# Latent attention on one core: each unit's value matmuls as a run of their own, ten runs a pair of heads in place of five

## What is computed

```python
def _L1_attn_ref(x, latent_w, latent_b, Wd_w, Wd_b, out_w, out_b):
    Wdkv = x @ latent_w + latent_b                                    # 36 latents per token: keys and values
    q = jnp.einsum('btc,hcl->bhtl', x, Wd_w) + Wd_b[None, :, None, :] # 16 heads
    scores = jnp.einsum('bhtl,bsl->bhts', q, Wdkv) / jnp.asarray(np.sqrt(d_head), dtype=x.dtype)
    scores = jnp.where(causal[None, None, :, :], scores, -jnp.inf)
    attn = jax.nn.softmax(scores, axis=-1)
    y = jnp.einsum('bhts,bsl->bhtl', attn, Wdkv)
    z = jnp.transpose(y, (0, 2, 1, 3)).reshape(b, t, h * Wdkv.shape[-1])
    return z @ out_w + out_b
...
x = x + _L1_attn_ref(_layernorm(x, axis=-1), L1_attn_latent_w, ...)
```

## Time and profile before

| | us |
|---|---|
| median of 3 runs | 3037.49 (3032.99 to 3039.72) |
| the profiled execution, its own time | 3026.82 |
| span of that execution in the trace | 3025.1 |
| latent attention's pairs and outputs in it | about 2061 to 2911 |
| granted clock of PE, mean, as a share of 2.4 GHz | 0.941 |

### The profile page before, as it was taken

The page is one execution under the profiler, slowest core; times in us unless marked ns, Lnnn a source line. Parts: engine busy times, 40 slices in busy tenths (PEclk is TensorE's granted clock), DMA queues, the critical chain, the costliest instruction groups (busy, mean ns, idle before and its releaser), DMA issues. The chain is left out here.

```text
span 3025.1 us, 53686 instructions
## 1 busy us (share of the span) xinstructions
PE 2700.4 (89%) x15208; PEld 1865.9 (62%) x15208; DVE 2011.5 (66%) x5083; ACT 1140.5 (38%) x2101; POOL 887.8 (29%) x1203
## 2 busy tenths in 40 slices
PE   7999999967887888779999999778998988999989
PEld 5888888844554555458888888534455455455454
DVE  6777777747778687667777777545655555556542
ACT  3111111116666666621111111234544544544544
POOL 3223223315655555532223233001111111111200
PEclk9999999968989889879999999888999999999999
DMA  3000000000000000020000000001110110111100
GB/s 137 0 0 0 0 0 0 0 1 2 3 3 3 3 3 2 2 101 1 0 0 0 0 0 1 1 4 45 37 37 26 37 37 26 37 37 28 46 2 28
DMA packets 31976, 52.01 MB, mean 17 GB/s; under 512 B 8178, under 2 KB 14066, under 8 KB 31732
## 3 DMA queue, kind: packets, MB, share of 16 engines
q1 hardware_dynamic: 27124, 41.88, 4.5%
q0 software_dynamic: 4608, 7.09, 0.9%
HBM read 17.93 MB, written 2.10 MB: 7 GB/s over the span
## 5 line engine op out<-in xcount | busy, mean ns | idle before, releaser
L616 DVE SCALAR_TENSOR_TENSOR moe_acc<-moe_ps,moe_comb,moe_acc 128x512 f32<-128x512 f32 x896 | 660.9, 744 | 155.1 <-PE moe_ps L322 152.1
L2221 DVE CUSTOM_DVE_ANT_0 attn_masked<-attn_psm,attn_causal 128x1024 f32<-128x1024 f32 (+1 forms) x504 | 363.1, 757 | 259.0 <-PE attn_psm L1903 258.4
L2118 ACT ACTIVATE attn_probs<-attn_pse 128x512 f32<-128x512 f32 (+1 forms) x640 | 314.1, 557 | 341.7 <-PE attn_pse L1918 339.3
L322 PE MATMUL moe_ps<-moe_Wg,moe_xh 128*128 128x512 f32 x1024 | 328.9, 403 | 19.0 <-DVE moe_Wg L539 19.0
L353 PE MATMUL moe_ps<-moe_Wd,moe_ih 128*128 128x512 f32 x1024 | 341.6, 415 | 3.4 <-DVE moe_Wd L539 3.4
L322 PE MATMUL moe_ps<-moe_Wu,moe_xh 128*128 128x512 f32 x1024 | 332.8, 406 | 3.1 <-POOL moe_Wu L477 3.1
L1830 POOL TENSOR_SCALAR_AFFINE_SELECT attn_probs<-attn_probs 128x256 f32<-128x256 f32 (+1 forms) x192 | 95.0, 495 | 709.1 <-ACT attn_probs L2118 709.0
L1934 PE MATMUL attn_psy<-attn_probs,attn_V 128*64 128x512 f32 (+3 forms) x1536 | 290.6, 508 | 0.0
L487 POOL TENSOR_SCALAR moe_part<-consts,moe_pick,moe_prob 128x8 f32<-128x8 f32 x256 | 97.4, 394 | 625.5 <-ACT moe_prob L410 625.5
L1115 POOL TENSOR_TENSOR attn_R<-attn_R 128x1024 f32<-128x1024 f32 (+1 forms) x128 | 213.6, 1680 | 188.4 <-DVE attn_R L1463 188.4
L1903 PE MATMUL attn_psm<-attn_kS,attn_qS 108*128 108x512 f32 (+3 forms) x672 | 197.9, 395 | 48.5 <-DVE attn_mx L2221 42.5
(11 more groups left out here) (228 smaller groups left out, 4755.7 us busy)
## 6 DMA issues: line engine op xcount, KB each, us to landing
attn_qS<-attn_qH SPq DMA_DIRECT2D x192, 72.0 KB
attn_qS<-attn_qL SPq DMA_DIRECT2D x96, 72.0 KB
attn_qS<-attn_qH POOLq DMA_DIRECT2D x64, 72.0 KB, 2.1
moe_stageg<-in_w_gate SPq DMA_DIRECT2D x8, 512.0 KB, 7.3
moe_stageu<-in_w_up SPq DMA_DIRECT2D x8, 512.0 KB, 7.2
moe_stageg<-in_w_down SPq DMA_DIRECT2D x8, 512.0 KB, 3.6
attn_qS<-attn_qL POOLq DMA_DIRECT2D x32, 72.0 KB, 2.5
out<-X SPq DMA_DIRECT2D x8, 256.0 KB, 2.4
```

The source lines that it names most:

```text
L322: last = pe.matmul(expert_bank[j % 4][:, :], a[q][:, :], w[b][:, cols], start=k == 0, stop=k == 2)
L616: dve.scalar_tensor_tensor(acc[:, q, r, :], expert_bank[j % 4][:, :], comb[:, q, r, e:e + 1], acc[:, q, r, :], ALU.mult, ALU.add).then_inc ...
L2118: act.activation(probs[:, ring(q, u), c, HALF - n:HALF], e_part(k, HALF - n, HALF), ACT.Exp, scale=SCORE_SCALE).then_inc(p_ready, 1)
L2221: dve.tensor_tensor_reduce(masked[:, 0 if j >= 4 else 1, 0:n], max_part(k, 0, n, spare), causal[:, SEQ - n:SEQ], 1.0, NEG, ALU.add, ALU.ma ...
```

## The change

A step's run of two units is parted. The unit of even number is put behind the step's first two scores, ahead of the third; the unit of odd number stays at the step's end. This holds for `d == 0` too, whose two units are those of the pair before (no such units where `i == 0`). In the last step that puts unit 6 ahead of the transpose and the projection, and leaves unit 7 behind them. Nothing is added or left out: the same matmuls on the same tiles with the same waits. The last pair of an element keeps units 8 and 9 behind unit 7.

```diff
-                        for u, c in ((2 * d, 0), (2 * d, 1), (2 * d + 1, 0)):
-                            scores(m, q, u, c)
+                        for c in range(2):
+                            scores(m, q, 2 * d, c)
+                        if d >= 1:
+                            values(m, q, 2 * d - 2)
+                        elif i > 0:
+                            values(m - 1, 1 - q, NU - 2)
+                        scores(m, q, 2 * d + 1, 0)
...
                         if d == 0:
                             if i > 0:
-                                for u in (NU - 2, NU - 1):
-                                    values(m - 1, 1 - q, u)
+                                values(m - 1, 1 - q, NU - 1)
...
                         else:
-                            for u in (2 * d - 2, 2 * d - 1):
-                                values(m, q, u)
+                            values(m, q, 2 * d - 1)
```

## The result

The changed kernel takes **3102.03 us** (median of 4 runs, 3096.98 to 3107.18) where the kernel before takes 3035.24 beside it: +66.8 us, a ratio of 1.0221 with a 95% interval of [1.0204, 1.0237]. Slower was forecast, by 56 us, at 3093 in a range of 3064 to 3120. The profiled execution took 3096.98, its span is 3095.2.

A forecast was written before the change was run, and what follows sets the result against it. PE's fixed order was taken to set the pace, with a DMA floor behind the transpose. Inner pairs gave 21 x 2.1 = 44 us, other pairs 4 + 4 + 4: +56 on 3026.8, plus 10.7 to the median, 3093 us; range 3064 to 3120.

The forecast's parts named there:

- A run's own price: On PE, each run of values costs 0.36 us besides its columns; 5 more runs an inner pair, 1.80 us.
- The Trainium skill's rule: Weight loads on PE overlap only matmuls of another row group; a run would add no 0.11, giving 3076 us.
- The walk: PE's changed order stepped from an inner pair's first scores: transpose at 21.3 in place of 19.20, +2.1 us a pair.
- The other terms: Elements' first, seventh and eighth pairs add 4 us each group; the very last pair adds 0.
- Unit 6: Moved from the transpose-to-scores part, which has a DMA floor, into the scores-to-transpose part: 0.85 us longer a pair.
- The floor behind the transpose: From transpose to next first scores, a DMA sets 3.5 to 3.8 us; the part does not get shorter.
- DVE keeping up: Rival: DVE keeps pace, PE loses its stops between scores and transpose; -15 us, 3022 us. Chance 0.06.
- About the same: Rival: waits hide half of the run prices and unit 6 costs nothing under the DMA; 3037 us. Chance 0.05.
- The clock: Rival: idle PE lowers its clock up to slot 1 in each pair, 40 us more, 3133 us. Chance 0.07.
- The last line of the chances: Closing chances for the whole kernel: slower (forecast and clock) 0.88, same 0.05, faster 0.07.
- new waits: PE waiting for DVE in an inner pair, chiefly ahead of slots 1 (0.81) and 3 (0.72): 1.65 us together.
- stops that go: Three old PE stops in an inner pair, at slots 2, 6 and the last scores, vanish: 2.2 us less.

The follow-up runs named there:

- short_middle: Kernel before with DVE reducing only 128 columns of each maximum tile and only steps 1 to 3 parted: 2995.18 us, ratio 0.9881.
- unit6: Kernel before with only the last step parted, unit 6 going ahead of unit 9's scores: 3060.61 us, +27.6 us, ratio 1.0093.
- pool_late: Changed kernel with POOL's three query DMAs issued behind its last mask of the pair: 3082.4 us, +49.4 us over the kernel before, ratio 1.0159.
- the short kernels: Kernel before and changed kernel, each with DVE reducing only 128 columns of each maximum tile: 2968.34 and 3035.0 us, +66.7 us between them.
- before_late: Kernel before with POOL's three query DMAs issued behind its last mask of the pair: 3023.05 against 3029.78 us, ratio 0.9980.
- new_order: Kernel before with PE's order rewritten as a list, 8 runs of values a pair in place of 5: 3008.0 us, -26.1 us, ratio 0.9912.

## Why the prediction was right, and by which step it was short

- **A run's own price**, 0.36 us: the joints stand at that price in the changed kernel and in short_middle, and a parting costs 0.28 net where hardly anything waits (short_middle). The mechanism holds; what a run frees elsewhere, the sum of joints left out.
- **The Trainium skill's rule** (TensorE: Matmul & The Clock Gate, section "Part 3: Packing small matmuls — row/col tiling"), that a weight load overlaps only with matmuls of another row group, would have made a run 0.11 cheaper; in the changed kernel too the two scores behind the DMA take 0.66 (2355.90 to 2356.56) where 0.47 would do, the bare load and the entry of a run again. The trace does not agree with the rule, and the changed kernel was slower than the 3076 that it gave, by more than the 10 us that the DMA adds (below). The total of short_middle alone could not have told: it fits 0.25 a run as well.
- **The walk** from first scores to transpose: slots 0 to 3 within 0.03 us, transpose 21.27 for 21.3. Waits ahead of slots 1 and 3, none at 2, 6 and at the last scores, all as walked.
- **The other terms**, 12 us for the first, seventh and eighth pairs of the elements: the trace's distances give 12.7. That it comes so near is luck in part: the three seventh pairs alone differ by -1.4, +2.3 and +2.5 us, at granted clocks of 0.81 to 0.90.
- **Unit 6**: its columns left the part that PE does not set and came into the one that it does. Right (unit6).
- **The floor behind the transpose** is the step that failed: "The part does not get shorter" held, but it got 0.37 us longer, 28 x 0.37 = 10 us, which is the difference between 56 and 66.8. The text said that SP's and POOL's queues keep their place relative to the transpose. They did not: with unit 6 behind them, unit 8's scores are earlier against the transpose, POOL's mask finishes 0.6 us earlier against it, and its query DMAs lead the small one by 0.39 us in place of 0.08, while SP issues that one 0.08 later. unit6 brings the loss and pool_late takes it away, and with it 8 us more that were not foreseen: even before the change this DMA landed later than it could.
- **Rivals.** DVE keeping up did not happen. "About the same" falls by unit6, whose move costs 27.6 us, and by the wait ahead of slot 1. The clock did not fall in each pair, though PE stands idle 1.4 us in each: 0.96 over the phase, 0.97 before. But two of the changed kernel's pairs of heads took about 27.2 us, at 0.94 and 0.87, and none of these did before; that is 4 us of the profiled execution, and what sets it off stays open. (The last line of the chances has 0.88 and 0.07 where the rivals' own add to 0.89 and 0.06.)
- **The account by cause**: the prediction gave 1.65 us a pair to new waits and 2.2 to stops that go, of which 0.6 is the last scores' wait for ACT. That made DVE look like a main part of the loss. By the short kernels its share in the sum is small, nothing by the times and 0.4 us a pair by the traces.

## What to carry to other kernels

Where one engine's program is a fixed order, moving a piece forward delays every consumer that is fed behind it: ask first which slot the piece now stands ahead of, then walk that engine and its single-buffered consumer for one period with distances from start to start. Work that lies under a latency that it does not set is free, so moving it out costs its whole length. And look at every queue whose trigger comes earlier against a small transfer on the critical path: here three larger ones ahead of it cost 18 us, by pool_late, more than the run prices of a whole step (32 runs of 0.36, 12 us).

## What the runs showed of the hardware that was not expected

- A DMA of 16 rows, 8 KB (`attn_ml`), landed 1.9 us after its issue when POOL's three 72 KB DMAs were issued behind it (pool_late, before_late), 2.3 when the first of them was issued 0.08 us ahead (before), 2.6 when 0.4 us ahead (the changed kernel) and 2.7 when 0.85 (new_order), on another queue in all cases. The lead alone does not decide it: in the last element of the kernel before it was 0.22 us, and five of the six landings took only 2.0 to 2.1. Why is not shown.
- Going from scores (`110*128`) to values (`128*64`) and back has a steady price: in the changed kernel's pair a full unit alone takes 1.01 us (2375.82 to 2376.83) and the 384 + 128 unit the same (2356.56 to 2357.57), as put together from runs of two before.
